# Attention scores as row-tile pairs, key transfers on POOL's queue, softmax sums read back after the second gelu

## The reference, cut to what matters

```python
x = _L0_cond_ref(x, cond, P, W, b)          # a rotation of x (16, 256, 288) in a 64-wide subspace
for layer in (1, 2, 3):                     # three transformer blocks, each on 16 x 256 x 288
    ada = silu(c) @ W_ada + b_ada           # 6 shifts, scales and gates for each batch
    h = layernorm(x) * (1 + scale) + shift
    q, k, v = h @ W_qkv + b_qkv             # 16 heads of width 18
    scores = einsum('bhnd,bhmd->bhnm', q, k) * 18 ** -0.5
    o = softmax(scores) @ v
    x = x + gate * (o @ W_proj + b_proj)
    h = layernorm(x) * (1 + scale2) + shift2
    x = x + gate2 * (gelu(h @ W_fc1 + b_fc1) @ W_fc2 + b_fc2)   # 288 -> 1152 -> 288
```

## Time and profile before

| | |
|---|---|
| time, median of 3 runs | 2103.05 us (2098.47 to 2103.8) |
| the profiled execution's own time | 2105.64 us |
| its span, first to last instruction | 2103.9 us |
| PE / PEld busy | 1967.8 / 1754.2 us (94% / 83%) |
| DVE, ACT, POOL busy | 1210.3, 1120.0, 1003.5 us (58%, 53%, 48%) |
| mean granted clock of PE | 0.969 |
| instructions | 49860 |

### The profile page before, as it was taken

How to read it: one execution, slowest core, us unless ns; L and a number is a source line. 1 busy time by engine, 2 the same in 40 slices (tenths; PEclk the granted TensorE clock), 3 DMA queues, 4 the chain that set the end, 5 groups by cost and what they waited for, 6 DMA issues and landing times. The chain is left out here.

```text
span 2103.9 us, 49860 instructions
## 1 busy us (share of the span) xinstructions
PE 1967.8 (94%) x16599; PEld 1754.2 (83%) x16599; DVE 1210.3 (58%) x2720; ACT 1120.0 (53%) x1932; POOL 1003.5 (48%) x1031
## 2 busy tenths in 40 slices
PE   4785799999999999899999999999999999999997
PEld 2553589999899988789899899998789998998986
DVE  6874466546556475556556465575565565564641
ACT  4232455564655645554655656645555656656552
POOL 1002345545455554645455454554655554554534
PEclk9797899999999999999999999999999999999998
DMA  6523443332333323432333323333433323333320
GB/s 171 139 79 118 126 117 87 100 99 80 104 89 94 99 78 105 146 106 78 108 93 90 95 84 105 97 82 101 137 89 90 98 81 106 96 90 93 86 80 26
DMA packets 138971, 207.34 MB, mean 99 GB/s; under 512 B 35700, under 2 KB 96274, under 8 KB 137822
## 3 DMA queue, kind: packets, MB, share of 16 engines
q1 hardware_dynamic: 111582, 169.78, 29.0%
q10 hardware_dynamic: 25040, 29.18, 4.9%
q0 software_dynamic: 2256, 7.17, 1.3%
HBM read 99.51 MB, written 20.82 MB: 57 GB/s over the span
## 5 line engine op out<-in xcount | busy, mean ns | idle before, releaser
L2070 DVE TENSOR_REDUCE maxima<-scores 128x4 f32<-128x1024 f32 x384 | 460.4, 1222 | 186.1 <-PE scores L1819 181.0
L1411 POOL TENSOR_TENSOR hidden<-g_full,hidden 128x512 fp32r<-128x512 f32 (+1 forms) x240 | 280.4, 1177 | 358.4 <-ACT hidden L1647 357.1
L1604 ACT ACTIVATE probs<-scores 128x1024 f32<-128x1024 f32 x384 | 383.1, 1027 | 95.4 <-PE pv_ps L1856 56.8
L1881 PE MATMUL mlp_ps<-h_mlp,w_up 128*128 128x256 f32 (+1 forms) x3024 | 410.0, 288 | 9.5 <-ACT hidden L1647 5.4
L1881 PEld LDWEIGHTS mlp_ps<-h_mlp,w_up 128*128 128x128 f32 (+1 forms) x3024 | 381.0, 190 | 40.4 <-issue 20.1
L1736 PE MATMUL mlp_ps<-w_down,hidden 128*128 128x288 f32 x2592 | 388.8, 295 | 0.0
L1736 PEld LDWEIGHTS mlp_ps<-w_down,hidden 128*128 128x128 f32 x2592 | 369.4, 188 | 18.1
L1819 PE MATMUL scores<-k_stack,q_stack 108*128 108x512 f32 x768 | 241.3, 406 | 20.8 <-DMA k_stack<-qk 18.2
L1842 PE MATMUL scores<-q_stack,k_stack 110*128 110x256 f32 x1536 | 245.7, 292 | 3.6 <-ACT probs L1604 2.4
L1842 PEld LDWEIGHTS scores<-q_stack,k_stack 110*128 110x128 f32 x1536 | 207.8, 191 | 32.5 <-issue 18.9
L1594 ACT ACTIVATE neg_max<-att_ps 16x256 fp32r<-16x256 f32 x48 | 17.9, 373 | 387.3 <-PE att_ps L1829 387.3
(11 more groups left out here) (230 smaller groups left out, 2849.6 us busy)
## 6 DMA issues: line engine op xcount, KB each, us to landing
q_stack<-qk SPq DMA_DIRECT2D x144, 180.0 KB
k_stack<-qk SPq DMA_DIRECT2D x288, 90.0 KB
inv_sum<-inv_scratch ACTq DMA_DIRECT2D x192, 128.0 KB, 2.6
k_stack<-qk SPq DMA_DIRECT2D x288, 54.0 KB
x_mid<-out_x SPq DMA_DIRECT2D x48, 288.0 KB, 4.2
out_x<-x_out SPq DMA_DIRECT2D x48, 288.0 KB, 3.1
x_in<-out_x SPq DMA_DIRECT2D x47, 288.0 KB, 3.9
q_stack<-qk SPq DMA_DIRECT2D x144, 72.0 KB
```

What stands on the lines that cost most here:

```text
L1411: tt(out, full, high.bitcast(F32), ALU.subtract).then_inc(signal, 1)
L1604: evict(probs[:, u % 4, :, :, :], scores[u % 2][:, :, :, :], ACT.Exp, scale=SCALE)\
L1881: last = mm(up_bank[n % 2][:, (m % 2) * T:(m % 2 + 1) * T], w[:, m * P:(m + 1) * P], h, start=count == 0, stop=count == 6)
L2070: nc.vector.tensor_reduce(out=maxima[:, :, :, u], in_=scores[u % 2][:, :, :, :], axis=AX.X, op=ALU.max).then_inc(s_max, 1)
```

## The change

1. The stacks hold one head at partitions 0 to 53 (3 terms x 18 channels) and the other at 64 to 117. `k_stack` loses its zero blocks and is half as wide. Each head's product is a row tile of 64 x 128 (`tile_position=(0, 0)` and `(64, 0)`), and the two heads' matmuls alternate. A unit takes 4 matmuls of 256 columns in the scores (before: 2 of 512) and 4 in the shifted scores, as before. The extra row with the maxima is row 54 of each head.
2. Units are computed two at a time (`score_units`, `shifted_units`: 8 matmuls). A pair waits for the reader of the pair before it, where a unit used to wait for the reader of the unit two before it. The pairs stand at other places among the MLP's products, and ACT's first exponentials come ahead of `qk_high(1)`.
3. Transfers: all are of one head, 18 partitions. SP issues 6 and 9 for `q_stack`; POOL issues 6 and 6 for `k_stack` (`first_keys`, `last_keys`), ahead of its `hidden_low` and, at b = 0, ahead of `low_weights("w_out")`.
4. ACT issues `load_sums` behind `gelu(it - 1, 1)`; before, it stood ahead of it.
5. With the stacks' new layout, the projection's columns are reordered (7 blocks for 6 in the weights' conversion), tiles 0 and 1 have 108 rows and the others 126 instead of the reverse, and the initial fill of `k_stack` on ACT is one instruction instead of six.

```diff
+        def head_into_stack(engine, stack, j, par, part, src, row, units, signal):
+            first = R * par + HD * j
+            engine.dma_start(stack[first:first + HD, units, :].bitcast(F32),
+                             qk[part][row:row + HD, src, :].bitcast(F32)).then_inc(signal, 16)
...
+            def first_keys(it, first=False):
+                pool.wait_ge(s_qk_lo, QK_USES * it + QK_USES)
+                pool.sem_inc(s_tick[1], 1)
+                if not first:
+                    pool.wait_ge(s_st, 8 * it - 3 + PRE)
+                    pool.sem_inc(s_tick[1], 1)
+                for j in range(3):
+                    for par in range(2):
+                        head_into_stack(pool, k_stack, j, par, K_PARTS[j], slice(0, 5), PAIR + HD * par, slice(0, 5), s_key_a)
+            def last_keys(it, first=False):
+                if not first:
+                    pool.wait_ge(s_st, 8 * it + PRE)
+                    pool.sem_inc(s_tick[1], 1)
+                for j in range(3):
+                    for par in range(2):
+                        head_into_stack(pool, k_stack, j, par, K_PARTS[j], slice(2, 5), 2 * PAIR + HD * par, slice(5, 8), s_key_b)
...
@@ ACT
-                for n in range(3):
-                    if after:
-                        qk_high(it + 1, n)
-                    if n < 2:
-                        exponentials(it, n)
+                if after:
+                    qk_high(it + 1, 0)
+                exponentials(it, 0)
+                exponentials(it, 1)
+                if after:
+                    qk_high(it + 1, 1)
+                    qk_high(it + 1, 2)
...
@@ PE
-            def score_unit(it, u):
-                if u == 0:
-                    pe.wait_ge(s_stack_a, PIECES_A * (it + 1) + 16)
-                if u == 5:
-                    pe.wait_ge(s_stack_b, PIECES_B * (it + 1) + 16)
-                if u < 2:
-                    pe.wait_ge(s_exp, 8 * it - 1 + u + PRE_EXP)
-                else:
-                    pe.wait_ge(s_max, 8 * it + u - 1)
-                r = slice(0, PAIR_ROWS)
-                for qt in range(2):
-                    last = mm(scores[u % 2][:, qt, :, :], q_stack[r, u, qt * P:(qt + 1) * P],
-                              k_stack[r, u, :, :], start=True, stop=True)
-                last.then_inc(s_score, 1)
+            def score_units(it, u):
+                if u == 0:
+                    pe.wait_ge(s_stack_a, PIECES_A * (it + 1) + 16)
+                    pe.wait_ge(s_key_a, KEYS * (it + 1))
+                    pe.wait_ge(s_exp, 8 * it + PRE_EXP)
+                else:
+                    pe.wait_ge(s_max, 8 * it + u)
+                if u == 4:
+                    pe.wait_ge(s_stack_b, PIECES_B * (it + 1) + 16)
+                    pe.wait_ge(s_key_b, KEYS * (it + 1))
+                for v in (u, u + 1):
+                    for qt in range(2):
+                        for par in range(2):
+                            r = slice(R * par, R * par + HEAD_ROWS)
+                            last = mm(scores[v % 2][:, par, qt, :], q_stack[r, v, qt * P:(qt + 1) * P],
+                                      k_stack[r, v, :], start=True, stop=True, tile_position=(R * par, 0))
+                    last.then_inc(s_score, 1)
...
@@ DVE
                 for u in range(8):
-                    if u == 3:
+                    if u == 4:
                         normalise(it)
-                    if u == 5 and before:
+                    if u == 6 and before:
                         gate_down(it - 1, 0)
```

More of the change, by code:

```diff
@@ L368, in constant_stacks @@
                     .then_inc(early["s_init"], 1)
[L369 to L380, removed]
+                A(k_stack[:, :, :].rearrange("p u t -> p (u t)"), one[:, 0:1].to_broadcast([P, H // 2 * T]), ACT.Copy)\
+                    .then_inc(early["s_kinit"], 1)
             def high_weights(n):
@@ L1304, in load_x_in @@
                 sp.dma_start(x_in[:, :, :], dram["out"][b]).then_inc(s_xin, 16)
-            def into_stack(j, part, src, rows, units, signal):
-                sp.dma_start(q_stack[PAIR * j:PAIR * j + PAIR, units, :].bitcast(F32),
-                             qk[part][rows, src, :].bitcast(F32)).then_inc(signal, 16)
-            def head_into_stack(j, par, part, src, row, units, signal, key=True):
-                dest = slice(PAIR * j + HD * par, PAIR * j + HD * par + HD)
-                stack = k_stack[dest, units, par, :] if key else q_stack[dest, units, :]
-                sp.dma_start(stack.bitcast(F32), qk[part][row:row + HD, src, :].bitcast(F32)).then_inc(signal, 16)
-            Q_PARTS, K_PARTS = (0, 1, 0), (0, 0, 1)
             def stacks(it, first=False):
@@ L1831, in maxima_transposes, with shifted_units @@
                 last.then_inc(s_max_ps, 1)
[L1833 removed]
+            def shifted_units(it, u):
                 if u == 0:
                     pe.wait_ge(s_neg_st, 32 * it + 32 + 16)
[L1837 to L1840 removed]
+                else:
+                    pe.wait_ge(s_exp, 8 * it + u + PRE_EXP)
+                for v in (u, u + 1):
                     for kt in range(2):
[L1842 to L1844 removed]
+                        for par in range(2):
+                            r = slice(R * par, R * par + HEAD_ROWS + 1)
+                            last = mm(scores[v % 2][:, par, kt, :], k_stack[r, v, kt * P:(kt + 1) * P],
+                                      q_stack[r, v, :], start=True, stop=True, tile_position=(R * par, 0))
+                    last.then_inc(s_st, 1)
             def weighted_values(it, g):
@@ L1914, in prologue @@
                 attention_transposes(1)
-                for u in range(8):
-                    score_unit(0, u)
+                for u in range(0, 8, 2):
+                    score_units(0, u)
             def half_step(l, b):
@@ L2069, in unit_max @@
                     dve.wait_ge(s_max_ps, it + PRE)
-                nc.vector.tensor_reduce(out=maxima[:, :, :, u], in_=scores[u % 2][:, :, :, :],
+                nc.vector.tensor_reduce(out=maxima[:, :, :, u].rearrange("p q r -> p r q"), in_=scores[u % 2][:, :, :, :],
                                         axis=AX.X, op=ALU.max).then_inc(s_max, 1)
```

93 lines of the change are left out of this document (44 added, 49 removed).

## The result

The changed kernel takes 2191.97 us (median of 4, 2188.59 to 2195.88) against 2102.91 us: a ratio of 1.043, interval 1.0405 to 1.0452. It is 4.3% slower where I had forecast 2070 us. Its profiled execution spans 2191.3 us, 87.4 more than before.

What follows compares the result with a forecast made beforehand. PE, 94% busy, was taken as the bound. Per half step -0.97 + 0.15 + 0.06 = -0.76 us, by 47: -36; with -9 and +12, 2105.64 became 2072.6, and 2070 us after a 2.6 us offset; range 2040 to 2150.

Steps and rivals of the forecast that it cites:

- 0.97 us off a half step: PE's own work: scores -0.16 us, shifted scores -0.71, and a gap of about 0.1 between `up(2)` and `up(3)` gone.
- 0.89 for seven pairs of the eight: On PE, a pair of units with a tiling switch at both ends: 0.48 + 0.41 = 0.89 us, against 0.93 before.
- the 0.15 us for the fourth pair: PE's fourth pair waits 0.15 us for maxima, since `normalise` (1.28 us) now stands between units 3 and 4.
- the 0.06 for `up(4)`: PE waits 0.06 us at `up(4)`, as POOL's twelve issues at 0.615 us each delay `hidden_low(0)` and `gelu(2)`.
- the place that I watched: POOL called the tight place: twelve issues ahead of `hidden_low(0)`, taken at 0.615 us each, with no slack behind them.
- the break-even: POOL's issue price of 0.61 us, above which each further 0.01 us costs 0.12 us in a half step.
- The rival with a dear issue: POOL's issue costs 0.67 us or more, delaying `hidden_low`, `gelu(2)` and `up(4)`; at 0.775 the time is 2164 us; chance 0.23.
- two other waits cost nothing: First keys issued by t = 17.6, needed at 22; last by 21.2, needed near 29: no cost to PE.
- is over by then: On ACT, `load_sums` behind `gelu(1)` is free: its wait for the stored sums ends while the gelu runs.
- the step that gave the second pair no wait: DVE takes 2.35 us for two maxima; PE has 2.4 to 2.6 us of `down` between pairs, so no wait.
- -9 and +12: Start: shorter key waits, -9 us. Layer ends: keys late behind `w_out` at b = 0, +11, and +1 at b = 1.
- the 2070 of the forecast: Whole kernel: 2070 us, with 2050 to 2090 given a chance of 0.52.

Runs made afterwards that it cites:

- e5: Changed kernel, all twelve of POOL's key transfers still issued but each carrying one unit instead of five or three, other keys left out: 2073.36 us, 0.9866.
- e6: Changed kernel with POOL's last six key transfers behind `hidden_low(1)` instead of ahead of `hidden_low(0)`: 2147.27 us, 1.0232.
- e2: Kernel before the change with one edit alone, `load_sums` behind `gelu(1)`: 2092.6 us, 0.9966.
- e1: Changed kernel with one edit undone, ACT issuing `load_sums` ahead of `gelu(1)` again: 2196.62 us, 1.0451.
- e4: Changed kernel with DVE's `inverse` behind the maxima of the first two units instead of ahead of all maxima: 2213.5 us, 1.0535.

## Why the prediction was wrong

- **PE's own work was right.** I summed 0.97 us off a half step; with the waits gone it is 37.81 - 36.73 = 1.08 us (median of e5). A pair with its switches costs 0.68 + 0.09 + 0.10 = 0.87 us, where I took 0.89 for seven pairs of the eight; 7 x 0.02 = 0.14 more than covers the difference. Of the two waits that I added, the 0.15 us for the fourth pair stands in no regular half step of e5, and the 0.06 for `up(4)` only in the three with POOL's stops (1.1 to 1.4 us there).
- **POOL's issue was right as the place that I watched, and not the bound.** It costs 0.516 us and not 0.615; `hidden_low(0)` starts before the break-even. The rival with a dear issue gave 2164 us, near the result, and did not happen.
- **The step that failed is "two other waits cost nothing", with the sentence that the wait for the stored sums "is over by then".** I priced the twelve transfers by the engine that issues them and by when their own data are needed. I never asked which other transfers are out at that time. The store of the sums is issued at t = 17.4, in the middle of them. Before the change the load could start 2.0 us behind it, and "over by then" holds only with such a number; but in that stretch the DMA engines now carry 173 GB/s and not 88. It became 4.5 us, and the load took 2.4 us in place of 1.7; `inverse` came 2.7 us later, at t = 24.5. The maxima, ahead of which DVE stood idle for 2.28 us before, start right behind it, at t = 22.1 in e5 and at 24.6 here. So the step that gave the second pair no wait, because DVE takes only 2.35 us for two maxima, failed with it: it waited in 30 of 33 regular half steps, and in none of e5. The other of the two waits, for the first keys, was not free either: 7.5 us in 15 of the 33, and 17.8 us in all.
- **Size.** The 33 regular half steps should have lost 33 x 1.08 = 36 us and took 51 more: 87 us of waits, lower clock and POOL's three stops. In e5 the same 33 take 1216 us, 32 less than before. Of the 83 us between the two, 62 are idle time of PE (65.9 us against 3.6): 40.1 for the maxima, 12.7 for gelus ahead of `up` (10.2 of it in the three half steps in which POOL stops), 7.5 for keys and 5.0 at `b_down`. The 23.9 us at half the clock cost some 12 more, an estimate. About 9 stay unplaced. So the late sums are the largest part of what I had missed, about half, and not all of it.
- **Start and layer ends.** I had -9 and +12. Ahead of the first half step the trace has 3 us less, but that varies between traces by as much. SP's fifteen queries take 16.3 us there beside POOL's keys, 1.08 each and not 0.70, and PE waits 7.9 us for them in place of the 11.3 us for keys; but its waits for maxima there and at the first transposes went from 2.2 to 8.1 us, and so most of the gain went. The first half step is 5.1 us longer (44.2 against 39.1), and again for the maxima: they cost 2.1, 2.0 and 5.1 us ahead of its second, third and fourth pair. Where nothing stands between two pairs, waiting for both maxima of the pair before costs 2.0 us, and waiting for a unit cost 0.5; the sum had no term for it. The 14 half steps at layer ends and at the start cost 36 us more. In e5 it is 6 us more, so the data make 30 of these 36. The 6, beside the gain of 14 x 1.08 = 15 that PE's work should give there, are 21 us of other losses where I had 12. In these half steps PE's score pairs wait 21.4 us for maxima in e5, and its units waited 1.5 before: the order in pairs makes nearly all of the 21.
- **Luck.** Without the data e5 gives 2073 us, next to the 2070 of the forecast, and part of this is luck. Its steady gain is larger than I said, its layer ends are worse, and its part ahead of the first half step is 7.9 us shorter than in the kernel before, of which PE's waits explain some 2. What I left out, the data of the keys beside the small transfers and beside each other, is worth 119 us.

With all its data, no version with the new pairs beats the kernel before; e6 comes nearest, at 1.023. The only edit here that beats the kernel before with all data in place is `load_sums` behind `gelu(1)` (e2), by 0.3%.

## What to carry to other kernels

A transfer has three prices: the issuing engine's time (here 0.516 us), its own landing (3.4 us at the median), and what it does to small transfers that are out at the same time (2.5 us for the store of the sums). When transfers are moved to a second queue, list the small ones with a waiting engine behind them (here sums out and back, inverse out and back), and compare GB/s in that stretch before and after. To test it, keep every issue and take only the bytes away: one such run (e5) showed what four runs with lines moved (e1 to e4) had not. It prices all that the bytes do, and not one wait alone.

A long-waiting instruction at the head of an in-order list (DVE's `inverse`) is harmless only as long as nothing behind it is ready. Moving ready work earlier can make an old wait into a new one.

## What was not expected of the hardware

- Row tiles of 64 x 128 in alternation start 0.003 us apart at the median and within 0.010 us in 95% of 1536 cases, and so do their loads; a pair of units with both switches costs 0.87 us for 8 matmuls of 256 columns.
- POOL's issue of a transfer from SBUF to SBUF takes 0.516 us where SP's takes 0.70 (queries, changed kernel) to 0.775 (keys, before) for transfers of the same 18 partitions.
- With POOL's and SP's transfers together, four packets of 0.16 us each started 2.7 to 3.6 us after their issue, although the 16 engines were busy for only 56% of the stretch from t = 17 to 22. Why they wait so long the traces do not show.
- In half steps 12, 28 and 43 (counted from 0), 192 and 180 of POOL's transfers apart, POOL stopped for 5 us after the eighth of twelve issues; in e5, with the same number and less data, for 2.6 to 2.8 us at the same places. Its cause was not tried.
